# Both linear layers, the mean and the batch statistics in strips of 62 nodes inside the first edge pass

## What is computed

```python
x = _layernorm(x + _L0_gnn_ref(x, edge_index, L0_gnn_W_self1, ...), axis=-1)      # the first half
x = _layernorm(x + _L1_gnn_ref(x, edge_index, edge_attr_96, L1_gnn_Wq, ...), axis=-1)
# _L0_gnn_ref:
deg = jax.ops.segment_sum(jnp.ones((src.shape[0],), x.dtype), dst, num_segments=n)
agg_sum = jax.ops.segment_sum(x[src], dst, num_segments=n)
h_mean = agg_sum / jnp.maximum(deg, 1.0)[:, None]
out1 = x @ W_self1 + h_mean @ W_neigh1
out1 = _batch_norm(out1, g1, beta1)                     # mean and variance over all nodes
hp = jax.nn.relu(x @ W_pool + b_pool)
agg_max = jax.ops.segment_max(hp[src], dst, num_segments=n)
h_max = jnp.where(deg[:, None] > 0, agg_max, 0.0)
out2 = x @ W_self2 + h_max @ W_neigh2
out2 = _batch_norm(out2, g2, beta2)
return jax.nn.leaky_relu(out1 + out2, negative_slope=LEAKY_SLOPE)
```

## Time and profile before

| | us |
|---|---|
| median of 3 runs | 4267.41 (4266.93 to 4277.27) |
| the profiled execution | 4270.08 |
| its span, first to last instruction | 4268.4 |
| first pass: first gather to last window addition | 8.22 to 2049.42 |
| from there to ACT's L502 | 2049.42 to 2100.05 |
| node blocks, to the first product of the second pass | 2100.05 to 2166.74 |
| second pass and last layer norm | 2166.74 to 4268.4 |

### The profile page before, as it was taken

How to read it: one execution, slowest core, us unless ns; L and a number is a source line. 1 busy time by engine, 2 the same in 40 slices (tenths; PEclk the granted TensorE clock), 3 DMA queues, 4 the chain that set the end, 5 groups by cost and what they waited for, 6 DMA issues and landing times.

```text
span 4268.4 us, 114391 instructions
## 1 busy us (share of the span) xinstructions
PE 3889.0 (91%) x31146; PEld 3381.9 (79%) x31146; DVE 2637.0 (62%) x9276; ACT 1449.3 (34%) x3823; POOL 3118.9 (73%) x3252
## 2 busy tenths in 40 slices
PE   7888888888888888888899999999999999999996
PEld 5777777777777777777589999999999999999996
DVE  6665555565555555555556666666666666666666
ACT  3333333333333333333343333333333333333333
POOL 7777777777777777777157777777777777777774
PEclk9999999999999999999899999999999999999997
DMA  3111111111111111111134444444444344443442
GB/s 90 40 39 40 39 39 40 39 39 40 39 39 40 39 39 39 39 39 39 47 110 117 116 116 116 116 116 116 116 116 116 116 116 116 116 116 116 116 116 78
DMA packets 209079, 333.36 MB, mean 78 GB/s; under 512 B 73181, under 2 KB 156824, under 8 KB 208952
## 3 DMA queue, kind: packets, MB, share of 16 engines
q0 software_dynamic: 129040, 238.05, 21.8%
q1 hardware_dynamic: 80008, 94.94, 7.7%
HBM read 325.49 MB, written 7.24 MB: 78 GB/s over the span
## 4 chain that ended last, share of the span: by engine, by line
PE 59%; POOL 19%; issue 13%; DMA 6%; DVE 2%; POOLq 1%; ACT 0%; DVEq 0%; SPq 0%; ACTq 0%
POOL kvg L394 19%; PE bank L1143 10%; PE bank L1121 10%; PE bank L1129 10%; PE bank L1138 9%; PE bank L1160 8%; DMA kvg<-in_x_dram,idx 6%; PE bank L989 3%; PE bank L1000 2%; PE bank L1011 2%; PE bank L1028 2%; PE bank L1152 2%; PE bank L991 1%; PE bank L1069 1%; PE bank L1070 1%
## 5 line engine op out<-in xcount | busy, mean ns | idle before, releaser
L394 POOL DMA_INDIRECT kvg<-kv_table,idx x1613 | 1556.3, 965 | 510.0 <-issue 389.3
L394 POOL DMA_INDIRECT kvg<-in_x_dram,idx x1613 | 1534.8, 952 | 497.0 <-issue 456.8
L643 DVE TENSOR_SCALAR S<-iotaW,rel 128x64 f32<-128x64 f32 x4848 | 894.2, 272 | 26.4 <-issue 26.2
L989 PE MATMUL bank<-ident,kvg 128*96 128x128 f32 x3232 | 449.9, 282 | 313.7 <-DMA kvg<-in_x_dram,idx 299.7
L668 DVE TENSOR_TENSOR acc<-acc,bank 97x64 f32 (+1 forms) x808 | 177.5, 220 | 802.3 <-PE bank L1011 510.2
L989 PEld LDWEIGHTS bank<-ident,kvg 128*96 128x96 f32 x3232 | 364.1, 163 | 379.2 <-DMA kvg<-in_x_dram,idx 268.8
L551 ACT COPY eaC<-bank 96x512 f32<-96x512 f32 x404 | 235.1, 582 | 1120.2 <-PE bank L1121 1117.6
L467 ACT COPY eaC<-bank 96x512 f32<-96x512 f32 x404 | 235.2, 582 | 982.7 <-DVE scan L658 972.0
L892 DVE COPY qwin<-bank 64x96 f32<-64x96 f32 x404 | 100.9, 250 | 681.1 <-PE bank L1160 468.3
L658 DVE TENSOR_TENSOR_SCAN scan<-keepC,scan,bank 96x512 f32<-96x512 bf16 x404 | 512.2, 1268 | 0.0
L1028 PEld LDWEIGHTS bank<-S,scanE 128*96 128x96 f32 x3232 | 339.0, 165 | 216.8 <-issue 215.1
(11 more groups left out here) (125 smaller groups left out, 4804.2 us busy)
## 6 DMA issues: line engine op xcount, KB each, us to landing
ea<-in_edge_attr_dram SPq DMA_DIRECT2D x402, 192.0 KB
kvg<-in_x_dram,idx POOLq DMA_INDIRECT x1613, 2.5
kvg<-kv_table,idx POOLq DMA_INDIRECT x1613
kv_table<-stage SPq DMA_DIRECT2D x6, 672.0 KB, 3.3
stage<-counts_row SPq DMA_DIRECT2D x1, 2352.0 KB, 12.9
xN<-in_x_dram SPq DMA_DIRECT2D x6, 336.0 KB, 3.5
out_dram<-xN SPq DMA_DIRECT2D x6, 336.0 KB
src_all<-in_src_groups_dram SPq DMA_DIRECT2D x1, 804.0 KB
```

The lines of the kernel that those rows point to most:

```text
L394: pool.indirect_dma_start(out=to[:, r, j, :], out_offset=None, in_=table, in_offset=bass.IndirectOffsetOnAxis(ap=idx[:, r, j:j + 1], axis= ...
L643: last = dve.tensor_scalar(S[:, r % R, n, :], iotaW[:, :], rel[:, bass.ds(i * R + r, 1), n // J, n % J:n % J + 1] .rearrange("p a b -> p ( ...
L989: pe.matmul(bank[0][0:D, j:GE:J], xg[:, r, j, 0:D], ident[:, :], start=True, stop=True)
```

## The change

A strip is 62 nodes (`SW`). Strip s is handled inside turn s + 3 (`LATE`) of the first pass, 98 strips (`NS`) in all. By then the windows have moved past its nodes: each strip's nodes end at least 62 nodes before the first target of the group that opens turn s + 2, for every strip of this data, and a new count (`count_early`, 98 numbers on one partition) raises the flag if that fails.

- Step r = 0 of the turn: PE multiplies a matrix `pick` (whose last row is ones) with the strip's sums and counts, which spreads the counts over 96 partitions (bank 6, columns 448 to 509); DVE takes their maximum with 1 into `share`.
- r = 1: PE does the second linear layer of the strip (two products, four instructions, since each float32 product counts as two); DVE inverts `share`, copies the layer's result into `acc[:, 1]` and takes its statistics.
- r = 2: DVE multiplies the strip's sums by `share`.
- r = 3: PE does the first linear layer of the strip; DVE copies and takes statistics.

All of this stands on PE just ahead of the group's `sums` products, on DVE just ahead of the sum window's addition. Behind the pass 174 nodes remain (`REST`); they go through the same steps once, and the statistics of 99 pieces instead of 14 are joined. The counts' way through DRAM is gone. The four weights of the linear layers are loaded after the third piece of x instead of after the last. The flag is formed in turn 4 instead of behind the pass. The first four loads of edge features (L307), which went out beside the linear layers, wait until the statistics are joined, since these now lie in their buffer.

```diff
@@ DVE, first pass @@
+                def strip_out(i, r):
+                    idle, s = own_strip(i, r)
+                    if idle:
+                        return
+                    piece = bank[6][0:D, S0:S0 + SW]
+                    dve.wait_ge(s_sum, ready(i, r))
+                    if r % R == 0:
+                        dve.tensor_scalar_max(share[:, 0:SW], piece, 1.0).then_inc(s_count, 1)
+                    elif r % R == 1:
+                        dve.wait_ge(s_count, s + 1)
+                        dve.reciprocal(share[:, 0:SW], share[:, 0:SW]).then_inc(s_share, 1)
+                    elif r % R == 2:
+                        a = acc[0:D, 0, strip(s)]
+                        dve.wait_ge(s_share, s + 1)
+                        dve.tensor_tensor(a, a, share[:, 0:SW], ALU.mult).then_inc(s_mean, 1)
+                    if r % R in (1, 3):
+                        m = 1 if r % R == 1 else 0
+                        dve.tensor_copy(acc[0:D, m, strip(s)], piece)
+                        dve.bn_stats(stats[:, m, bass.ds(s, 1), :].rearrange("p a c -> p (a c)"), piece
+                                     ).then_inc(s_stat, 1)
...
                     if live(r - 1):
                         features(i, r - 1)
+                        strip_out(i, r - 1)
+                        flag_out(i, r - 1)
                         add_window(r - 1, DSUM, 0, s_sum, s_acc)
@@ PE, first pass @@
+                    if r == 0:
+                        pe.matmul(piece, pick[:, :], acc[0:DSUM, 0, strip(s)],
+                                  start=True, stop=True)
+                    elif r == 1:
+                        pe.wait_ge(s_w, 64)
+                        pe.wait_ge(s_accm, freed(i, r, R + 1))
+                        pe.matmul(piece, w_self2[:, :], xT[0:D, strip(s)], start=True, stop=False)
+                        pe.matmul(piece, w_neigh2[:, :], acc[0:D, 1, strip(s)], start=False, stop=True)
+                    elif r == 3:
+                        pe.wait_ge(s_mean, s + 1)
+                        pe.matmul(piece, w_self1[:, :], xT[0:D, strip(s)], start=True, stop=False)
+                        pe.matmul(piece, w_neigh1[:, :], acc[0:D, 0, strip(s)], start=False, stop=True)
...
+                    strip_in(i, r)
@@ DVE, behind the pass (both linear layers, their chunks and the counts' way are removed) @@
+            rest = acc[0:D, 0, NS * SW:N]
+            dve.wait_ge(s_countR, 1)
+            dve.tensor_scalar_max(share_rest, bank[0][0:D, 0:REST], 1.0).then_inc(s_shareR, 1)
+            dve.wait_ge(s_shareR, 1)
+            dve.reciprocal(share_rest, share_rest).then_inc(s_shareR, 1)
+            dve.wait_ge(s_shareR, 2)
+            dve.tensor_tensor(rest, rest, share_rest, ALU.mult).then_inc(s_meanR, 1)
+            dve.wait_ge(s_stat, 2 * NS)
+            for n, m in enumerate((1, 0)):
+                dve.wait_ge(s_linR, n + 1)
+                dve.bn_stats(stats[:, m, NS, :], bank[1 + n][0:D, 0:REST]).then_inc(s_statR, 1)
+                dve.wait_ge(s_statR, n + 1)
+                step(dve.bn_aggr(mv[:, m, :], stats[:, m, :, :].rearrange("p n c -> p (n c)")))
```

More of the change, by code:

```diff
@@ L43 @@
 KV_BANKS = (6, 7, 4, 5)
+SW = N // TURNS + 1
+LATE = 3
+NS = TURNS - LATE
+REST = N - NS * SW
+S0 = 512 - W
 DSUM = D + 1
@@ L115, in build @@
         warm = sb("warm", [1, 1])
-        stats = sb("stats", [D, 2, NCH, 6])
+        limit = sb("limit", [1, NS])
+        share = sb("share", [D, W])
+        pick = sb("pick", [DSUM, D])
         mv = sb("mv", [D, 2, 2])
@@ L236, in own_tiles, with own_strip, strip @@
             return range(0) if g < 0 else range(min(g * TRANS, NT), min((g + 1) * TRANS, NT))
+        def own_strip(i, r):
+            t = i + r // R
+            return isinstance(t, int) and not LATE <= t < TURNS, t - LATE
+        def strip(s):
+            return bass.ds(s * SW, SW)
         def irregular(eng):
@@ L482, in _ @@
             pipeline(act, turn1, 2)
[L485 to L494, removed]
+            rest = bass.ds(NS * SW, REST)
+            for n, m in enumerate((1, 0)):
+                act.wait_ge(s_statR, n + 1)
+                act.copy(acc[0:D, m, rest], bank[1 + n][0:D, 0:REST]).then_inc(s_copyR, 1)
             act.wait_ge(s_bn, 1)
@@ L615, in _ @@
             dve.memset(eps_col[:, 1:2], 0.0)
+            dve.memset(pick[0:D, :], 0.0)
+            dve.memset(pick[D:DSUM, :], 1.0)
             dve.memset(ones_col[:, :], 1.0).then_inc(s_ones, 1)
@@ L726, in _ @@
                 dve.sem_inc(s_made0, 1)
-            dve.sem_inc(s_deg, 1)
+                dve.sem_inc(s_stripG, 1)
+                with dve.Fori(0, NS) as s:
+                    a = acc[0:D, 0, strip(s)]
+                    dve.wait_ge(s_countG, s + 1)
+                    dve.tensor_scalar_max(share[:, 0:SW], bank[0][0:D, 0:SW], 1.0).then_inc(s_shareG, 1)
+                    dve.wait_ge(s_shareG, s * 2 + 1)
+                    dve.reciprocal(share[:, 0:SW], share[:, 0:SW]).then_inc(s_shareG, 1)
+                    dve.wait_ge(s_shareG, s * 2 + 2)
+                    dve.tensor_tensor(a, a, share[:, 0:SW], ALU.mult).then_inc(s_meanG, 1)
+                    dve.wait_ge(s_linG, s + 1)
+                    for n, m in enumerate((1, 0)):
+                        dve.tensor_copy(acc[0:D, m, strip(s)], bank[1 + n][0:D, 0:SW])
+                        last = dve.bn_stats(stats[:, m, bass.ds(s, 1), :].rearrange("p a c -> p (a c)"),
+                                            bank[1 + n][0:D, 0:SW])
+                    last.then_inc(s_stripG, 1)
@@ new lines, in _ @@
+                pe.wait_ge(s_stripG, NS + 1)
+            rest = bass.ds(NS * SW, REST)
+            pe.matmul(bank[0][0:D, 0:REST], pick[:, :], acc[0:DSUM, 0, rest],
+                      start=True, stop=True).then_inc(s_countR, 1)
+            pe.matmul(bank[1][0:D, 0:REST], w_self2[:, :], xT[0:D, rest], start=True, stop=False)
+            pe.matmul(bank[1][0:D, 0:REST], w_neigh2[:, :], acc[0:D, 1, rest], start=False, stop=True
+                      ).then_inc(s_linR, 1)
+            pe.matmul(bank[2][0:D, 0:REST], w_self1[:, :], xT[0:D, rest], start=True, stop=False)
@@ L1076, in stay_warm @@
+            pe.wait_ge(s_meanR, 1)
+            pe.matmul(bank[2][0:D, 0:REST], w_neigh1[:, :], acc[0:D, 0, rest], start=False, stop=True
+                      ).then_inc(s_linR, 1)
             def stay_warm(times, b):
```

132 lines of the change are left out of this document (59 added, 73 removed).

## The result

The changed kernel takes 4332.74 us (median of 4 runs, 4328.4 to 4337.67), the kernel before 4267.54 beside it: a ratio of 1.015, 95% interval [1.0137, 1.0163]. It is 65 us slower. The forecast was 4312, 45 slower, with a range of 4256 to 4352.

The account below looks back on a forecast made before the run. POOL's gathers pace the first pass; strips lengthen a two-group loop through PE, DVE and ACT beyond them. Terms +80.4 + 1.5 + 1.1 - 38.2 = +44.8 on the median of 4267.41 give 4312 us, range 4256 to 4352.

Parts of the forecast that it names:

- What bounds the pass: First pass: POOL's gathers set the pace, 20.00 us a turn or 10.00 for two groups, with a loop behind them.
- the hidden loop over two groups: First pass: chain through PE, DVE and ACT back to PE's front(g+2), 8.87 or 8.93 us against POOL's 10.00.
- The size of the loop: First pass with strips: steps of 10.40 and 10.44, together 20.84 a turn; excess taken as 0.82, 80.4 us over 98 turns.
- Turns 3 to 5 and the end of the pass: First pass: strips and transposes together add another 1.5 us; the last strip's unhidden delay adds 1.1.
- PE's clock in the pass: First pass, PE: the prediction's sum has no term for falls of the granted clock.
- Between the passes: Last window addition to node blocks: 50.63 us becomes about 12.4, saving 38.2 (between 36 and 43).
- Rival A: First pass: POOL stays at 20.00 a turn and strips disappear in the waits; 4232 us, chance 0.12.
- The port between DVE and POOL: First pass, r = 2: strip product delays a gather, at most 98 x 0.3 = 29, so 4262; a quarter of A's chance.
- Rival B: First pass: part of the strips' work hides, excess 0.30 to 0.49 a turn; 4256 to 4280 us, chance 0.14.
- C: First pass, DVE: load waits until strip operations have ended, about 0.55 more a turn; 4365 us, chance 0.08.
- B's other half: First pass, PE: the strip's products take 0.36 us, where the sum took 0.42.

Follow-up runs that it names:

- the load ahead of the wait: Changed kernel with DVE loading the sum window's first node ahead of the wait for sums, before the strip's operations: 4222.46 us, ratio 0.9896 to the kernel before.
- DVE's operations alone: Changed kernel without PE's strip products in the first pass; DVE does all strip operations on columns 0 to 61 of the bank: 4272.36 us.
- two loads: Kernel before, without strips, with the sum window's first node loaded twice behind the wait for sums in every group: 4337.34 us, ratio 1.0171.
- both places filled: Changed kernel with two dummy PE products of 128 columns behind `back` in every second group, ahead of front of r = 1 and r = 3: 4303.23 us.
- one place alone: Changed kernel with the two dummy PE products only ahead of front of r = 3, 4331.16 us, or only ahead of r = 1, 4333.66 us.

## Why the prediction was right, and where it was short

**What bounds the pass**: right. POOL paced it before, the hidden loop over two groups stood 1.10 below it, and the slack measured without strips lies between 0.82 and 1.42, by estimate at 1.08.

**The size of the loop**: right to 0.04, in part by luck. The two steps together measured 20.80 where the sum gave 20.84 (0.82 taken for the excess, 0.80 measured, +78 in place of +80.4), and the step from r = 1 to r = 3 measured 10.38 against 10.40. Of its parts r = 1 on DVE was 1.22 (1.15), and r = 3 1.06 (1.09), the copy at 1008.24 to the addition at 1009.30 in the timeline. But PE's products added only 0.31 from front to the end of sums (4.06 against 3.75), where 0.42 was taken and 0.36 was the low end; in r = 1 the 0.11 more on DVE than the 1.11 of the sum made up for it, and in r = 3 a maximum window that came 1.13 behind the sum window (1009.30 to 1010.43), where 0.94 to 1.01 had been read. The 0.06 for each instruction that passes the queue is in no row; the runs show only the 1.22 and the 1.06 that it went into. That the odd groups and the even groups form two loops, which was argued from the code and the rows, is now shown by moving one layer.

**Turns 3 to 5 and the end of the pass**: wrong in size, both. For the three turns the sum has 1.5 and three times 0.82, 4.0; the fronts show 0.4. There the copy of x had put the load behind a wait in the kernel before too (0.81), so it couldn't be paid again, and in r = 3 of the changed kernel copy and window still stand 0.81 apart, with the strip's operations between them:

```profile
102.83 0.55 DVE L686 COPY xT<-bank 96x384 f32<-96x384 f32 x1 [0.85 <-PE bank L1075]
...
103.64 0.22 DVE L680 TENSOR_TENSOR acc<-acc,bank 97x64 f32 x1
```

For the end 1.1 was forecast and 2.6 measured. The granted clock had fallen there before the pass was over (0.50 from 2153 to 2157), where the kernel before still had 0.96 (from 2046 to 2050).

**PE's clock in the pass**: missing, and the main step that failed. The sum took the granted clock of 1.00 of rows 1 for granted and asked only how long PE works, not how its waits would lie. They were one regular wait of 0.7 ahead of each front; in the new rhythm they are shorter and come in clusters, 18 falls come with it, and +30 us with them; what sets off a single fall stays open. With that term the sum would have been 4342; 4333 was measured. That 4333 lies in the range is luck in this respect: the range's upper part stood for a larger excess of the loop, not for the clock.

**Between the passes**: right, 12.02 against 12.4. The joins took 2.83 each against 3.1, the reciprocal 1.24 as forecast.

**Rival A, the cover holds**: 4232 was its time, and it is what the version with the load ahead of the wait does, 4222. The mechanism was priced right; it needed the load's place. The Trainium skill, "Perfetto Trace Analysis", section Identifying the Most-Contended Engine, would look to the engine with the highest occupancy. No run here bears that out for DVE: it was busier in the fast version (996.93 of 1500) than in the slow one (315.62 of 500), and what held the slow one up was 0.48 and 0.70 of idle time on DVE.

**The port between DVE and POOL**: no cost of the size that was set aside. In the fast version each strip product began 0.05 to 0.25 behind the start of a gather, in all of 75 turns looked at, and these gathers took 0.94 or 0.95. In the version with the layer moved to r = 2, 17 gathers began inside a strip product, and they took 0.94 to 0.97, where 0.3 more had been reckoned; one of them:

```profile
1010.46 0.22 DVE L702 TENSOR_TENSOR acc<-acc,share 96x62 f32 x1 [0.70 <-PE bank L1075]
...
1010.62 0.94 POOL L409 DMA_INDIRECT kvg<-in_x_dram,idx  x1 [0.30 <-PE bank L1075]
```

The Trainium skill, "SBUF — State Buffer", section Who interferes with whom, says that a VectorE instruction with two inputs in SBUF contends with a GpSimd instruction that reads SBUF. The second pass agrees, with its 1.24, but what is paid there depends on how much of the product is left: in the kernel before, gathers that began with 0.42 of L902 to go took 1.24, and two with 0.18 to go took 1.00. A strip product is 0.22 in all.

**Rival B** (part hides) and **C** (the load waits for the strip's operations): out by the 1.22, which is longer than what B needs (below 1.0) and shorter than C's 1.7. B's other half, PE's products at 0.36, was nearer than the 0.42 of the sum.

## What to carry to other kernels

Before adding work to an engine that looks idle, close the loops: follow the work from one instruction round over the other engines back to its next turn, and compare that length with what paces now; the difference is the cover, and it is shared by all that stands in the same loop, not by all that stands on the same engine. Here a register load that stood ahead of a wait was free until another wait was put in front of it; keep such a load where it was (here 110 us, the falls of the clock included), and only then count the length of the new operations. Where a pass loses its pacemaker, look at how the waits of TensorE lie afterwards, and at the granted clock in short stretches, not in the sum.

## What the runs showed of the hardware that was not expected

The clock of TensorE fell to its lower level for moments in the loop of the changed kernel, and not in the loop of the kernel before; each fall cost a turn 1.67. How busy PE was doesn't sort the versions: the clock fell at 1326.98 of 1500 (DVE's operations alone), and didn't at 1320.38 (two loads), 1334.29 (the load ahead of the wait) or 1401.07 (both places filled). It fell behind waits of 0.24, 0.29 and 0.52, or of 0.53 and 0.46, close together, in 18 of the many turns that have them, and didn't behind regular ones of 0.7. Two dummy products a place, at both places, gave 29 us back; at one place alone nothing.

A second load of a register, right behind the first and behind the same wait, cost 0.60, the first 0.82.

The join of statistics grows with its length by 2.83 - 0.55 for 594 - 84 numbers, 4.5 ns a number, so that 99 small pieces cost 2.3 more than 14 large ones, in each of two joins.
